# Routing of batch 0 beside the fourth to sixth attention group, and its scatters between GpSimd's masks

## The chip, the core and the metric

The kernel runs on one core of a Trainium2 chip. The core has TensorE (PE; PEld is its weight load), VectorE (DVE), ScalarE (ACT), GpSimd (POOL) and SyncE (SP), each with a queue of its own that it works through in order; they wait for each other by semaphores, and 16 DMA engines move data. The metric is the device time of one execution in microseconds.

## The reference

Two transformer blocks on x of 2 x 1024 tokens by 128 channels, all in float32. The change touches the first block alone:

```python
h = _layernorm(x, axis=-1) * (1 + ca) + sa
x = x + ga * _L0_attn_ref(h, ...)      # causal attention, 16 heads of 8
h = _layernorm(x, axis=-1) * (1 + cb) + sb
x = x + gb * _L0_ffn_ref(h, ...)       # mixture of experts
# in _L0_ffn_ref, T = 2048 tokens, E = 64 experts of 128 -> 64 -> 128:
scores = jax.nn.sigmoid(x @ gate_w.T) + gate_bias
group_scores = scores.reshape(T, 8, 8).max(axis=-1)
_, sel_groups = lax.top_k(group_scores, 4)
topk_w, topk_i = lax.top_k(scores * mask, 6)
topk_w = topk_w / (topk_w.sum(axis=-1, keepdims=True) + 1e-08)
# out = shared expert + sum over the 6 experts of topk_w * down(silu(gate) * up)
```

The second block is four RWKV layers and a small mixture of experts, and is the same in both kernels.

## The kernel before

**Attention.** Batch and heads are cut into NG = 8 groups of 4 heads: groups 0 to 3 are batch 0, 4 to 7 are batch 1. A group is NU = 24 units. A unit takes one block of 128 keys, two heads and one half (c = 0 or 1) of the queries: TensorE forms scores (L808), ScalarE exp into pt, a ring of four (L1066), GpSimd masks the diagonal block where there is one (`mask`, L725: units 0 to 7 and 16 to 23 of a group), and after each second unit TensorE multiplies with V (`outputs`, L824) for the pair of units before. Beside the units of one group run the row maxima of the next: 38 pieces ("fills") of TensorE (L786, L790), each reduced by VectorE (L1218). Pieces take turns in three PSUM banks (4, 5, 7): `ITEMS` lists all users of these banks in order, the place modulo 3 gives the bank, and `await_bank` makes TensorE wait until the item three places before has been read. The last maxima are those of group 7, and end at unit 163 (unit 24g + u counts through, 0 to 191).

**Routing.** Tokens are handled in chunks of 512: chunks 0, 1 are batch 0, chunks 2, 3 batch 1. For a chunk: `inverse` (ScalarE, 1/den by Ln and Exp), `normalise` (VectorE), `project` with WO (TensorE), `add_attention`, `centre`, `square`, `variances`, `rstds`, `modulated`, `logits`, `exponentials`, then on VectorE `route_scores`, `route_groups`, `route_mask`, `route_top`, `route_comb`, whose operations each wait for the one before (`link`); `turn_h` and `keep_h` transpose h to tokens. Per batch follow `positions` (on TensorE counts of tokens per expert and ranks; on VectorE each token's six slot rows), `experts_of_tiles`, and the scatter: 8 blocks x 6 indirect DMAs of 64 KB on GpSimd (L735) that write h rows to their slots in memory.

In the kernel before all of this for chunks 0 and 1 is written beside the units of group 7 (`beside`, `last_group`), `positions(0)` after attention, and the scatters of both batches behind the last mask in GpSimd's queue.

**After attention** come the rest of routing, the shared expert (L894 to L903, L1415, L1419), 16 `slot_weights` of three operations (L1386 to L1389) on VectorE, and the experts: 28 quads of 4 x 128 slots per batch. A quad passes through `turn_rows` (L910), `gates` (L924), silu, moe_hid (L1426), `turn_hidden` (L933) and `downs` (L941) in four successive steps. The loads of a batch's quads wait for all its 48 scatters. Then outputs are gathered (L746) and combined.

## Time and profile before

| | us |
|---|---|
| median of 3 runs (lowest, highest) | 1055.51 (1054.58, 1059.43) |
| profiled execution, its own time | 1065.52 |
| span of its trace | 1063.8 |
| TensorE busy (share) | 879.5 (83%) |
| VectorE | 726.7 (68%) |
| ScalarE | 565.1 (53%) |
| GpSimd | 252.4 (24%) |
| first exponential of group 7, last product of attention | 287.1, 324.4 |
| scatters, first and last start | 331.7, 455.0 |
| gathers, first and last start | 498.5, 648.1 |

How to read the rows below. A row of a window gives from:to, its length, the busy time of each engine it names with the number of instructions (x), then the granted TensorE clock as a share of 2.4 GHz, the share of the DMA engines and GB/s. A row of the timeline gives start, duration, engine, line, operation, output<-input with shapes and how many were merged (x), and in brackets how long the engine had been idle before it and what ended that; "issue" is a gap for which the profile shows no wait. A row by source line has the shortest, middle and longest duration in ns. Durations of matmuls overlap their successors.

### The profile page before, as it was taken

Reading aid. Unit: us, or ns where it says so; the run is one execution under the profiler, and the core shown is the slowest. Engines: PE = TensorE matmul, PEld = TensorE weight load, DVE = VectorE, ACT = ScalarE, POOL = GpSimd, SP = SyncE. Lnnn points to the kernel's source line nnn. Section 1 sums busy time; section 2 is a strip of 40 time slices with the busy share of each in tenths; the row PEclk is TensorE's granted clock in tenths of the full one; section 3 lists DMA queues with packets and bytes.
Section 4 is the critical chain, followed back from the end, with each engine's and each line's share of the span. In section 5 each row is a group of like instructions: output and inputs, shape, how many; then the busy total and the mean of one; then the engine's idle time right before and its main releaser. Section 6 shows DMA issues by size and latency. Waiting matters only on the chain. (4 is left out here: it accounts for less than half of the span.)

```text
span 1063.8 us, 13432 instructions
## 1 busy us (share of the span) xinstructions
PE 879.5 (83%) x4333; PEld 453.7 (43%) x4333; DVE 726.7 (68%) x1323; ACT 565.1 (53%) x888; POOL 252.4 (24%) x348
## 2 busy tenths in 40 slices
PE   6899999999885527998999003869999999998998
PEld 3453344444222216887888001324433433343433
DVE  4879788888476576332655133679889888996675
ACT  3325666666762103553554001668769868875743
POOL 1011122222114777711770674000000000000000
PEclk9889899999986577998999555989999999998999
DMA  2732655642022124654774211100000020000001
GB/s 86 225 69 52 185 161 168 194 145 69 12 65 89 49 72 158 228 182 153 216 227 138 64 52 57 33 0 1 10 23 10 1 52 1 0 1 0 1 0 40
DMA packets 51054, 87.48 MB, mean 82 GB/s; under 512 B 11202, under 2 KB 22832, under 8 KB 49200
## 3 DMA queue, kind: packets, MB, share of 16 engines
q1 hardware_dynamic: 36716, 58.56, 18.6%
q10 hardware_dynamic: 8128, 15.47, 4.0%
q0 software_dynamic: 6144, 12.60, 3.7%
q8 instruction: 38, 0.62, 0.2%
q14 instruction: 28, 0.23, 0.1%
HBM read 43.28 MB, written 40.89 MB: 79 GB/s over the span
## 5 line engine op out<-in xcount | busy, mean ns | idle before, releaser
L1066 ACT ACTIVATE pt<-psum 128x1024 f32<-128x1024 f32 (+1 forms) x192 | 149.9, 814 | 115.6 <-PE psum L808 115.2
L1218 DVE TENSOR_REDUCE part_max<-psum 128x1 f32<-128x512 f32 (+3 forms) x304 | 184.5, 657 | 35.7 <-PE psum L790 19.9
L786 PE MATMUL psum<-ka,qa 72*128 72x512 bf16 (+3 forms) x384 | 115.1, 341 | 5.3 <-DVE part_max L1218 1.8
L746 POOL DMA_INDIRECT part<-slot_y,slot_row x96 | 92.9, 968 | 100.1 <-DMA slot_y<-pt 71.5
L735 POOL DMA_INDIRECT slot_x<-va,slot_row x96 | 95.4, 994 | 37.5 <-issue 29.0
L725 POOL TENSOR_SCALAR_AFFINE_SELECT pt<-pt 128x256 f32<-128x256 f32 x128 | 51.9, 407 | 220.0 <-ACT pt L1066 219.3
L808 PE MATMUL psum<-qa,ka 75*128 75x512 bf16 (+3 forms) x384 | 96.3, 334 | 3.1 <-DMA qa<-neg_t 1.5
L1426 DVE TENSOR_TENSOR moe_hid<-moe_silu,psum 128x256 f32<-128x256 f32 x56 | 23.3, 418 | 95.8 <-ACT moe_silu L1186 91.4
L824 PE MATMUL psum<-pt,va_g 128*32 128x512 f32 (+3 forms) x768 | 84.1, 511 | 0.4 <-POOL pt L725 0.3
L110 ACT ACTIVATE ln_sq<-psum 128x512 f32<-128x512 f32 x44 | 26.1, 594 | 100.4 <-PE psum L93 100.3
L786 PEld LDWEIGHTS psum<-ka,qa 72*128 72x128 bf16 x384 | 37.4, 98 | 81.1 <-DVE part_max L1218 59.6
L1193 ACT COPY pt<-psum 128x512 f32<-128x512 f32 x56 | 32.8, 585 | 62.4 <-PE psum L941 62.4
L941 PE MATMUL psum<-ka,moe_hid_t 64*128 x448 | 64.2, 284 | 0.0
L924 PE MATMUL psum<-qa,xs_t 128*128 x448 | 63.0, 286 | 0.0
L1763 PE MATMUL psum<-mix_c,wt_c 128*128 128x512 f32 x128 | 61.1, 600 | 0.0
L941 PEld LDWEIGHTS psum<-ka,moe_hid_t 64*128 64x128 f32 x448 | 53.9, 187 | 10.9 <-issue 10.9
L101 PE MATMUL psum<-ln_sq,mean 128*128 128x512 f32 x88 | 49.1, 653 | 11.4 <-ACT ln_sq L110 11.4
L924 PEld LDWEIGHTS psum<-qa,xs_t 128*128 128x128 f32 x448 | 57.7, 202 | 0.6 <-issue 0.3
L1773 PE MATMUL psum<-kf,wt_c 128*128 128x512 f32 x128 | 57.9, 594 | 0.0
L948 PE MATMUL psum<-ident,va 128*128 128x128 f32 x16 | 3.3, 357 | 65.4 <-DVE va L1443 65.4
L910 PE MATMUL psum<-ident,pt 128*128 128x128 f32 x224 | 39.3, 303 | 20.8 <-DMA pt<-slot_x 20.8
L1720 PE MATMUL psum<-hp,wt_a 128*128 128x512 f32 x96 | 50.0, 602 | 2.7 <-issue 2.7
(316 smaller groups left out, 1658.2 us busy)
## 6 DMA issues: line engine op xcount, KB each, us to landing
slot_x<-zero ACTq DMA_DIRECT2D x8, 1792.0 KB, 6.7
pt<-slot_x SPq DMA_DIRECT2D x56, 256.0 KB
slot_y<-pt SPq DMA_DIRECT2D x56, 256.0 KB, 2.1
qa<-in_moe_gu SPq DMA_DIRECT2D x4, 1024.0 KB, 5.8
qa<-rows_q SPq DMA_DIRECT2D x21, 192.0 KB
ka<-rows_k SPq DMA_DIRECT2D x21, 192.0 KB
wt_c<-in_channel_w SPq DMA_DIRECT2D x4, 576.0 KB, 4.0
o_den<-acc SPq DMA_DIRECT2D x32, 64.0 KB, 2.3
```

Of the source, the lines that this page charges most:

```text
L725: pool.affine_select(out=pt[:, u % 4, :, 0:P], in_=pt[:, u % 4, :, 0:P], compare_op=ALU.is_ge, fill=0.0, base=0, pattern=[[0, 2], [1, P]], ...
L735: pool.indirect_dma_start(out=xs_d[b], out_offset=bass.IndirectOffsetOnAxis(ap=row[:, n, j:j + 1], axis=0), in_=h_tok[:, n, :], in_offset= ...
L746: pool.indirect_dma_start(out=yg[:, n % 4, j, :], out_offset=None, in_=ys_d[b], in_offset=bass.IndirectOffsetOnAxis(ap=row[:, n, j:j + 1], ...
L786: mm = pe.matmul(bank[:, nk * h:nk * (h + 1)], qa[0:ROWS, g % RING, h0 + h, chunk(i, P)], ka[0:ROWS, g % RING, h0 + h, k0:k0 + nk], start= ...
L808: mm = pe.matmul(out[:, 0:n], ka[0:ROWS + 3, g % RING, 2 * p + k, chunk(j, P)], qa[0:ROWS + 3, g % RING, 2 * p + k, q0:q0 + n], start=True ...
L824: mm = pe.matmul(acc_bank[32 * h:32 * h + 32, q0 - CH * c:CH], va_g[k][:, j, h, :], pt[:, 2 * (q % 2) + h // 2, h % 2, 0:n], start=(j == 0 ...
L924: mm = pe.matmul(gu_bank[n % 2][:, chunk(k, P)], xs_t[:, n % 2, chunk(k, P)], gu_w[:, bass.ds(held[n][k], P)], start=True, stop=True)
L941: mm = pe.matmul(y_bank[n % 2][:, chunk(k, P)], hid_t[:, n % 2, chunk(k, P)], down_w[:, bass.ds(held[n][k], P)], start=True, stop=True)
L1066: act.activation(pt[:, u % 4, :, 0:n], score_bank[u % 2][:, :, 0:n], ACT.Exp, scale=SCALE)\
L1218: dve.tensor_reduce(part_max[:, h0:h0 + heads, slot], bank_of("fill", f)[:, 0:heads * nk].rearrange("p (h n) -> p h n", h=heads), AX_X, AL ...
L1763: pe.matmul(G.bank[6 + j % 2][:, :], wt_c[u // 2 % 2][:, WCK + j, :], mix_c[:, 0, q, :], start=True, stop=True)\
L1773: mm = pe.matmul(G.bank[4 + q][:, :], wt_c[u // 2 % 2][:, WCV + j, :], kf[:, j, q, :], start=(j == 0), stop=(j == 3), skip_group_check=True)
```

## The change

Batch 0 is routed beside groups 3 to 5. A table STEP_AT gives each of its 13 TensorE steps a unit (90 to 136), and the steps are entered in ITEMS, so that they take their turns in the banks of the row maxima; `await_bank` learns what frees each. VectorE and ScalarE have a `first_batch(unit)` with their parts of each step. ScalarE copies the centred chunk out of its bank first (one copy of 128x512 more for chunks 0 and 1). `positions` is split into `tile_ends`, `slot_keys` and `slot_rows`. GpSimd issues one scatter of batch 0 in each of the units 134 to 181, behind that unit's mask if there is one. `slot_weights` moves into the experts of batch 0, one in each second step.

```diff
+    EARLY = NU * 3
+    STEP_AT = {("project", 0): EARLY + 18, ("centre", 0): EARLY + 20, ("variance", 0): EARLY + 22, ("logits", 0): EARLY + 25,
...
+    SCATTER_AT = EARLY + 62
...
-        ITEMS += [("fill", f) for f in BACK[unit]]
+        ITEMS += [("fill", f) for f in BACK[unit]] + [item for item, at in STEP_AT.items() if at == unit]
...
+            if was == "project":
+                pe.wait_ge(x_new, k + 1)
+            if was == "centre":
+                pe.wait_ge(ln.squared, n0 + k + 1)
+                pe.wait_ge(centre_kept, k + 1)
+            if was == "variance":
+                pe.wait_ge(ln.logged, n0 + k + 1)
...
@@ GpSimd
+                        if 0 <= NU * g + u - SCATTER_AT < INDEXED:
+                            scatter(0, NU * g + u - SCATTER_AT)
-                for b in range(B):
-                    scatter(b)
+                for k in range(NU * NG - SCATTER_AT, INDEXED):
+                    scatter(0, k)
+                for k in range(INDEXED):
+                    scatter(1, k)
...
@@ TensorE, group(g)
+                        first_batch(unit)
                         beside(unit - NU * LAST)
...
                 def after_attention():
 
-                    positions(0)
+                    pe.wait_ge(v_in, NG)
                     turn_h(2)
-                    turn_experts(0)
                     project(3)
...
@@ ScalarE
+                    if c < 2:
+                        act.copy(G.h[:, chunk(c)], centre_bank[c][:, :]).then_inc(centre_kept, 1)
...
@@ VectorE
+                def first_batch(unit):
+
+                    for c in range(2):
+                        if unit == STEP_AT["project", c] - 1:
+                            normalise(c)
+                        if unit == STEP_AT["project", c]:
+                            add_attention(c)
+                        if unit == STEP_AT["variance", c] + 1:
+                            modulated(c)
+                        if unit == STEP_AT["logits", c] + 1:
+                            route_scores(c)
+                        if unit == STEP_AT["logits", c] + 4:
+                            route_groups(c)
+                        if unit == STEP_AT["logits", c] + 6:
+                            route_mask(c)
+                        if unit == STEP_AT["logits", c] + 8:
+                            route_top(c)
+                        if unit == STEP_AT["logits", c] + 10:
+                            route_comb(c)
+                    if unit == STEP_AT["count", 0]:
+                        tile_ends(0)
+                    if unit == STEP_AT["rank", 0]:
+                        slot_keys(0)
+                    if unit == SCATTER_AT - 2:
+                        slot_rows(0)
...
                 def after_attention():
 
-                    positions(0)
-                    experts_of_tiles(0)
                     route_scores(2)
...
-                    for n in range(NT):
-                        slot_weights(n)
...
                                 keep_hidden(n - 2)
+                            if not b and step % 2:
+                                slot_weights(step // 2)
```

GpSimd's queue in the kernel before, from the masks of group 6 on (affine_select is the mask, DMA the scatter or gather):

```order
L725 AFFINE_SELECT pt<-pt 128x2x128 x16
L718 COPY va_g<-va 128x256
L725 AFFINE_SELECT pt<-pt 128x2x128 x24
L735 DMA slot_x<-va,slot_row 14336x128 x96
L746 DMA part<-slot_y,slot_row 128x128 x96
```

The same queue in the changed kernel, from the copy of V in group 5 on:

```order
L746 COPY va_g<-va 128x256
L763 DMA slot_x<-va,slot_row 14336x128 x2
L753 AFFINE_SELECT pt<-pt 128x2x128
L763 DMA slot_x<-va,slot_row 14336x128
L753 AFFINE_SELECT pt<-pt 128x2x128
L763 DMA slot_x<-va,slot_row 14336x128
L753 AFFINE_SELECT pt<-pt 128x2x128
```

A scatter stands behind each mask; 16 such pairs, then nine scatters in a row, 16 pairs, and the last scatters follow.

VectorE's queue in the kernel before in group 4, where the row maxima (L1218) of the next group follow each other:

```order
L1248 COPY neg_t<-psum 96x128
L1218 TENSOR_REDUCE part_max<-psum 128x1 x12
L1218 TENSOR_REDUCE part_max<-psum 128x4
L1218 TENSOR_REDUCE part_max<-psum 128x1 x4
L1218 TENSOR_REDUCE part_max<-psum 128x2 x2
L1218 TENSOR_REDUCE part_max<-psum 128x1 x16
```

The same place in the changed kernel (row maxima are L1254), units 95 to 101:

```order
L1284 COPY neg_t<-psum 96x128
L1254 TENSOR_REDUCE part_max<-psum 128x1 x7
L1321 SCALAR_TENSOR_TENSOR h<-h,mod,ln_rs 128x512
L1324 TENSOR_SCALAR h<-h,mod 128x512
L1254 TENSOR_REDUCE part_max<-psum 128x1 x4
L1339 TENSOR_SCALAR score<-score 128x256
L1340 RECIPROCAL score<-score 128x256
L1341 TENSOR_TENSOR score<-score,gate_bias 128x256
L1254 TENSOR_REDUCE part_max<-psum 128x1
L1254 TENSOR_REDUCE part_max<-psum 128x4
L1254 TENSOR_REDUCE part_max<-psum 128x1 x3
L1346 TENSOR_REDUCE gmax<-score 128x4x8
```

Two to three operations of the routing now stand between every few maxima.

## Rows read from the trace of the kernel before

**Rows 1.** windows, all engines: a steady group, the stretches of routing, group 7, experts

```profile
170.50:199.20 28.70, 28.67 (x233) 11.80 (x225) 24.43 (x45) 19.38 (x27) 7.07 (x17) 1.00 0.57 182
...
190.20:246.60 56.40, 56.34 (x446) 23.45 (x448) 47.94 (x87) 37.84 (x52) 13.74 (x33) 1.00 0.44 135
...
297.50:324.40 26.90, 22.69 (x133) 7.79 (x133) 18.64 (x83) 17.18 (x25) 3.20 (x8) 0.86 0.02 7
...
416.00:494.00 78.00, 78.00 (x624) 69.71 (x623) 26.75 (x53) 39.32 (x76) 30.56 (x32) 1.00 0.55 184
```

**Rows 2.** timeline, between attention's end and the experts' first steps

```profile
328.84 0.63 ACT L1082 ACTIVATE rden<-rden 128x512 f32<-128x512 f32 x1
...
333.85 0.69 DVE L1252 TENSOR_TENSOR o_den<-o_den,rden 128x512 f32<-128x512 f32 x1
...
381.81 0.75 DVE L1419 SCALAR_TENSOR_TENSOR x<-psum,mod,x 128x512 f32<-128x512 f32 x1 [1.22 <-PE psum L903]
...
411.56 1.06 PE L933 MATMUL psum<-ident,moe_hid 128*64 128x128 f32 x4 [7.89 <-DVE moe_hid L1426]
...
415.97 1.21 PE L941 MATMUL psum<-ka,moe_hid_t 64*128 x8
...
419.03 1.16 PE L941 MATMUL psum<-ka,moe_hid_t 64*128 x8
```

**Rows 3.** timeline of GpSimd, and its scatters by source line

```profile
190.21 0.41 POOL L725 TENSOR_SCALAR_AFFINE_SELECT pt<-pt 128x256 f32<-128x256 f32 x1 [0.51 <-ACT pt L1066]
...
246.60 0.41 POOL L725 TENSOR_SCALAR_AFFINE_SELECT pt<-pt 128x256 f32<-128x256 f32 x1 [11.16 <-ACT pt L1066]
...
263.45 0.64 POOL L718 COPY va_g<-va 128x256 f32<-128x256 f32 x1
...
296.86 0.47 POOL L725 TENSOR_SCALAR_AFFINE_SELECT pt<-pt 128x256 f32<-128x256 f32 x1 [0.35 <-ACT pt L1066]
...
333.13 0.97 POOL L735 DMA_INDIRECT slot_x<-va,slot_row  x1 [0.30 <-issue]
...
L735 POOL DMA_INDIRECT slot_x<-va,slot_row x96: 963/967/1457, 331.7 to 455.0; - x96
```

**Rows 4.** windows and timeline of VectorE: routing, row maxima, steps of a chunk

```profile
297.08:305.67 8.59, 8.05 (x40) 1.00 0.12 32
...
325.00:331.36 6.36, 5.20 (x25) 0.77 0.66 231
...
261.74 5.92 DVE L1218 TENSOR_REDUCE part_max<-psum 128x1 f32<-128x512 f32 x10
...
275.52 0.69 DVE L1218 TENSOR_REDUCE part_max<-psum 128x1 f32<-128x512 f32 x1 [0.38 <-PE psum L790]
...
278.10 0.68 DVE L1252 TENSOR_TENSOR o_den<-o_den,rden 128x512 f32<-128x512 f32 x1
...
282.20 0.75 DVE L1274 SCALAR_TENSOR_TENSOR x<-psum,mod,x 128x512 f32<-128x512 f32 x1 [3.42 <-PE psum L840]
...
293.18 0.75 DVE L1281 SCALAR_TENSOR_TENSOR h<-psum,mod,ln_rs 128x512 f32<-128x512 f32 x1 [7.50 <-ACT ln_rs L1096]
...
293.97 0.49 DVE L1284 TENSOR_SCALAR h<-h,mod 128x512 f32<-128x512 f32 x1
```

**Rows 5.** timeline of TensorE in group 7

```profile
309.11 1.10 PE L840 MATMUL psum<-o_den,wo_t 128*128 128x512 f32 x2 [2.64 <-DVE o_den L1252]
```

**Rows 6.** timeline of VectorE: slot weights, and its idle time in the experts

```profile
382.47 0.55 DVE L1386 TENSOR_TENSOR same_key<-slot_key,top_key 128x384 f32<-128x384 f32 x1
...
384.24 0.56 DVE L1386 TENSOR_TENSOR same_key<-slot_key,top_key 128x384 f32<-128x384 f32 x1
...
425.12 0.42 DVE L1426 TENSOR_TENSOR moe_hid<-moe_silu,psum 128x256 f32<-128x256 f32 x1 [1.99 <-ACT moe_silu L1186]
```

**Rows 7.** windows of TensorE alone, in groups 0 and 1

```profile
76.00:79.00 3.00, 2.33 (x22) 1.00 0.03 6
...
106.00:109.00 3.00, 1.76 (x11) 0.99 0.53 136
```

More of the change, by code:

```diff
@@ L493, in stage_core @@
     FRONT[8], BACK[8] = beside_unit[8], []
+    EARLY = NU * 3
+    STEP_AT = {("project", 0): EARLY + 18, ("centre", 0): EARLY + 20, ("variance", 0): EARLY + 22, ("logits", 0): EARLY + 25,
+               ("turn_h", 0): EARLY + 27, ("project", 1): EARLY + 36, ("centre", 1): EARLY + 38, ("variance", 1): EARLY + 40,
+               ("logits", 1): EARLY + 44, ("turn_h", 1): EARLY + 46, ("count", 0): EARLY + 56, ("rank", 0): EARLY + 57,
+               ("experts", 0): EARLY + 64}
+    SCATTER_AT = EARLY + 62
     ITEMS = [("fill", f) for f in range(HEAD - 3)] + [("turn", 0)] + [("fill", f) for f in range(HEAD - 3, HEAD)]
@@ L862, in turn_h, with counts @@
                     mm.then_inc(turned, 1)
-                def positions(b):
+                def counts(b):
                     pe.wait_ge(picked_done, 2 * b + 2)
                     pe.wait_ge(const_done, 4)
-                    pe.wait_ge(prob_done, NU * NG)
                     tiles = range(BLOCKS * b, BLOCKS * (b + 1))
@@ L873, in positions, with ranks @@
                     mm.then_inc(count_psum, 1)
+                def ranks(b):
+                    tiles = range(BLOCKS * b, BLOCKS * (b + 1))
                     pe.matmul(rank_bank[b][:, :], earlier[:, :], picked[:, tiles[0]:tiles[-1] + 1, :].rearrange("p n e -> p (n e)"),
@@ L983, in beside @@
                     if w == 19:
-                        pe.wait_ge(exp_done, 2)
                         variances(2)
-                    if w == 21:
-                        pe.wait_ge(h_kept, 1)
-                        turn_h(1)
                     if w == 23:
                         logits(2)
+                def first_batch(unit):
+                    for c in range(2):
+                        if unit == STEP_AT["project", c]:
+                            await_bank(pe, "project", c)
+                            project(c)
+                        if unit == STEP_AT["centre", c]:
+                            await_bank(pe, "centre", c)
+                            centre(c)
+                        if unit == STEP_AT["variance", c]:
+                            await_bank(pe, "variance", c)
+                            variances(c)
+                        if unit == STEP_AT["logits", c]:
+                            await_bank(pe, "logits", c)
+                            logits(c)
+                        if unit == STEP_AT["turn_h", c]:
+                            await_bank(pe, "turn_h", c)
+                            pe.wait_ge(v_in, NG // 2)
+                            turn_h(c)
+                    if unit == STEP_AT["count", 0]:
+                        await_bank(pe, "count", 0)
+                        counts(0)
+                    if unit == STEP_AT["rank", 0]:
+                        await_bank(pe, "rank", 0)
+                        ranks(0)
+                    if unit == STEP_AT["experts", 0]:
+                        await_bank(pe, "experts", 0)
+                        turn_experts(0)
                 def group(g):
@@ L1020, in after_attention @@
                     turn_h(3)
-                    positions(1)
+                    pe.wait_ge(prob_done, NU * NG)
+                    counts(1)
+                    ranks(1)
                     turn_experts(1)
@@ L1145, in beside, with first_batch @@
                         rstds(2)
-                    if w == 22:
-                        keep_h(1)
+                def first_batch(unit):
+                    for c in range(2):
+                        if unit == STEP_AT["project", c] - 2 - 2 * c:
+                            inverse(c)
+                        if unit == STEP_AT["centre", c]:
+                            square(c)
+                        if unit == STEP_AT["variance", c]:
+                            rstds(c)
+                        if unit == STEP_AT["logits", c]:
+                            exponentials(c)
+                        if unit == STEP_AT["turn_h", c]:
+                            keep_h(c)
                 def group(g):
@@ L1269, in group @@
                         fills(BACK[unit])
+                        first_batch(unit)
                 def add_attention(c):
@@ L1467, in after_attention @@
                     route_comb(3)
-                    positions(1)
+                    tile_ends(1)
+                    slot_keys(1)
+                    slot_rows(1)
                     experts_of_tiles(1)
```

132 lines of the change are left out of this document (53 added, 79 removed).

## The prediction

> **What bounds the kernel now.** I read the engines' busy time by stage first, then the timeline around the joints of the stages, then one line at a time. A group of attention takes 28.7 us in its steady part, and TensorE is busy for 28.67 of it, at the full clock of 2.4 GHz (granted 1.00); VectorE is busy 24.43 and GpSimd 7.07 [rows 1]. So TensorE bounds groups 2 to 6, but VectorE has only 4.3 us of air in each. Group 7 has no row maxima left, and its last 16 units (297.5 to 324.4) are slower than TensorE's work asks: 22.69 busy of 26.90 [rows 1]. After attention comes the stretch in which nothing is near full: 324.4 to 416, where TensorE waits for the routing of chunk 3, then for the scatters of batch 0 (48 on GpSimd, then 48 of batch 1), and at last 7.89 us for moe_hid, because VectorE is still at the 16 slot weights [rows 2]. The first down projection starts at 415.97, and from there the experts run at 3.0 us a quad with TensorE 78.00 of 78.00 busy [rows 1, 2]. All that follows (batch 1, its gathers, the RWKV layers) hangs on that start. The question is thus: what does the change do to the end of attention, and to the distance from there to the first down projection.
>
> I count units through: unit 24g + u. A unit with a mask shows its time by GpSimd's mask: unit 89 at 190.21, unit 136 at 246.60, unit 175 at 296.86 [rows 3].
>
> **Part A, units 89 to 136: batch 0's routing beside the row maxima.** This window is 56.4 us now, TensorE 56.34 busy, VectorE 47.94 [rows 1]. What VectorE gets on top, for each of two chunks: the multiplication by 1/den 0.68, add_attention 0.75, modulated 0.75 + 0.49 and the small gaps, together 2.7; the routing chain 8.59 (it has links: each piece waits for the one before) [rows 4]. That is 5.4 + 17.2. Then counts, keys, rows and experts_of_tiles: 6.36 with a wait of 0.7 in it, so 5.6, and 0.3 to keep the expert numbers. Sum 28.5. With 47.9 this is 76.4 us of VectorE in a window of 56.4. Against it stand two things: maxima that now stand alone with 0.69 run at 0.592 when they queue (5.92 for ten) [rows 4], which I put at 2 us in the window; and VectorE's waits for the steps it shares with the others (13 banks of the ring of three go to steps, each held until ScalarE or VectorE has read it, and add_attention, modulated, the counts and the ranks are waited for in order), some 0.3 us each, 4 us. The ring lets TensorE be only three banks, about 1.8 us, ahead of VectorE, so a chain of 2.6 us that stands in one unit can't be hidden and must be paid out of the 4.3 us a group. Result 76.4 - 2 + 4 = 78.4, that is +22. TensorE's own new work here is six products of 128x512 at 1.10 [rows 5], and for transposes, logits, counts and ranks (an estimate from the same row by their columns) some 3 us, less what overlaps: about 9.2 us, and it lies under VectorE's. ScalarE, with 19.38 busy of 28.70 in a group [rows 1], has room for its eight operations of about 0.6 a chunk. Ends: if packing gave 4 us and no step waited, +16; if TensorE's 9.2 stood in series with VectorE's 76.4, +29. I take +22, by the busy row.
>
> **Part B, units 136 to 175: GpSimd.** Now 50.3 us from mask to mask (296.86 - 246.60). GpSimd then has, between these two starts, 39 scatters, 31 masks and one copy of V. A scatter is 0.967 and starts 0.30 after the one before, 1.27 in all; a mask is 0.41, the copy 0.64 [rows 3]. 39 x 1.27 + 31 x 0.41 + 0.64 = 62.9, +12.6. GpSimd becomes the bound here: masks are waited for by the output products, the pt ring holds four units, and TensorE and ScalarE can't run past it; in the eight units without a mask GpSimd still needs 10.2 for eight scatters and starts them late, so it gets no rest there. No row shows a mask next to a scatter. From below: the 0.30 vanishes when something else is in between, 39 x 0.97 + 13.3 = 51.1, +0.9. From above: mask and copy also get 0.30 behind them, 32 x 0.30 = 9.6 more, +22. I take 1.27 and 0.41, as both stand in rows.
>
> The Trainium skill (GPSIMD Engine Reference, section 2.1 Instruction dispatch) says that a Pool core starts its share of the next instruction as soon as it has done its own of the one before; by that rule alone the lower end, +0.9, would be the sum. It is a rival below, priced by rows.
>
> **Part C, units 176 to the end of group 7.** Routing of chunks 0 and 1 is gone from here. TensorE idles 4.2 us in 26.9 [rows 1]; 2.64 of it is the wait for the product with 1/den of chunk 2, which VectorE reached late because of chunk 1's chain [rows 5]; the transposes of chunks 0 and 1 go too. The clock falls to 1.2 GHz in this group now, behind that stall (0.86 granted in the window [rows 1]), and I expect one fall with the change too, behind the slow first half of the group. -4.5; ends 0 and -7.
>
> **Part D, end of attention to first down projection.** VectorE no longer starts with positions and experts of batch 0. The next thing in the way is 1/den of chunk 3: ScalarE ends it at 328.84 + 0.63 = 329.5, and it hangs on a DMA of the last accumulator, so it doesn't move; VectorE used it at 333.85 [rows 2]. So the chain of chunk 3 (project, centre, variance, logits, routing, rows, shared expert) moves by 4.35, not by the 6.4 removed. The shared expert's last addition, 381.81 + 0.75 = 382.6, comes at 378.2. Then TensorE can start on the experts at once: scatters of batch 0 are out before attention ends, the quads are loaded, and the slot weights have moved into the loop. Three steps to the first down projection: at most 3 x 3.06 (415.97 to 419.03 [rows 2]), less since the first steps are short; I take 8. 386.2 against 415.97: -29.8. Ends -27 (steps at 1.2 GHz) and -32. What covers the slot weights: three operations in 1.77 us (382.47 to 384.24) every second step, in VectorE's idle of 1.99 before moe_hid [rows 6]; if this cover failed by 0.5 us a time it would cost 7. Batch 1's scatters start with its rows, 4.35 earlier, last 61, and are done at half of batch 0's experts (28 x 3.0 = 84), so no new wait follows; the 39 us that they ran beside the experts until now (416 to 455 [rows 3]) left the steps at 3.0. Everything behind keeps its length.
>
> **Sum.** +22.0 + 12.6 - 4.5 - 29.8 = +0.3 us. The profiled execution took 1065.52 (span 1063.8); with the change 1065.8. The runs' median is 1055.51, 10 lower; moved by the same, 1055.8, say 1056. About 0.5% (5.3 us) is what a measurement of this kernel can tell from no change.
>
> **The rivals.**
> 1. Forecast: the two new bounds (VectorE to unit 136, GpSimd after it) eat what the earlier start gives. 1050 to 1063 by the ends of A alone. 0.40.
> 2. Mask and scatter overlap: 0.97 + 0.41 a pair. B is +0.9 instead of +12.6, 1056 - 11.7 = 1044. For it: a gap that is issue may lie under a mask that runs. Against it: each scatter behind another has its 0.30, as issue time and not as a wait [rows 3]. 0.22. The rule of the Trainium skill above would give this one.
> 3. Row maxima and routing share VectorE better than I think, and only TensorE's 9.2 us count in A: 1056 - 12.8 = 1043. Against it stand 76.4 us of work in 56.4. 0.10.
> 4. Slower: every GpSimd instruction carries the 0.30, a pair costs 1.98 us in units 136 to 175, which is 9.6 more: 1066. It decides from a mean of some 1.85 us a pair. 0.20.
> 5. Slower by the clock: in Part B TensorE is busy about 0.7 of the time in group 6. Rows show it staying at 1.00 with 2.33 of 3.00 busy, and falling after a stretch with 1.76 of 3.00 [rows 7]. At 1.2 GHz a unit with maxima costs 2 x 28.67 / 24 = 2.4 us, above GpSimd's 1.68; two such episodes of 6 us cost 6: 1062. 0.08.
>
> The chances: faster by over 0.5%: 2 and 3 nearly whole (0.29) and a little of 1 (0.03), 0.32. Slower: 4 and 5 (0.25) and 0.04 of 1, 0.29. Within: 0.39. The range, 1042 to 1068, reaches to the rivals on both sides; the likeliest case has 1050 to 1063 for itself.
>
> **What would show it.** A: mask of unit 136 (the first mask behind two scatters) near 269 instead of 246.6, VectorE over 90% busy before it and maxima without waits. B: 63 us from there to the last mask of group 7's first half, GpSimd above 90% busy, start of scatter to start of the next in masked units 1.68; 1.4 or 2.0 speaks for 2 or 4. A granted clock of 0.5 in group 6 speaks for 5. C and D: last output product near 354, first down projection near 416, and no wait for moe_hid at it. I am wrong if the first down projection moves by more than 5 us in either direction, or if steps of the experts with slot weights take over 3.1 us.

## The result and the profile after

The changed kernel takes 1068.46 us (median; 1064.76 the lowest) against 1055.05 for the kernel before on the same chip: ratio 1.0101, 95% interval [1.0057, 1.0146]. Medians here and below are of all executions, while ratios leave out those in a second, slower state (here one of the changed kernel, 1082.46 us), so a ratio isn't the quotient of the two medians. The changed kernel is slower by about 1%, which is 10.7 us; on the 1055.51 of the prediction that makes 1066, inside the range and near its upper end of 1068. The sum had said no change.

The profiled execution of the changed kernel took 1066.5 us (span 1064.8), 1.0 more than that of before (1065.52). The traces differ by less than the times because the profiled execution of before was a long one (1065.52 against a median of 1055). A second profile of the kernel before (run e0 below) took 1062.0. Both have stretches that the other lacks, and I give both. The places are those of the prediction, read from the timeline of GpSimd (masks) and of TensorE (products):

| stretch, us | before | e0 | after | forecast against before | measured against before, e0 |
|---|---|---|---|---|---|
| A, mask of unit 89 to that of 136 | 56.4 | 56.4 | 87.7 | +22 | +31.3, +31.3 |
| B, unit 136 to 175 | 50.3 | 50.2 | 60.0 | +12.6 | +9.8, +9.8 |
| C, unit 175 to the last output product | 27.0 | 24.0 | 23.0 | -4.5 | -4.0, -1.0 |
| D, from there to the first down projection | 92.1 | 89.0 | 59.7 | -29.8 | -32.4, -29.3 |
| from there to the end | 647.8 | 645.0 | 647.0 | 0 | -0.8, +2.0 |
| start to unit 89 | 190.2 | 195.7 | 187.3 | 0 | -2.9, -8.3 |
| from unit 89 to the end | 873.6 | 864.6 | 877.5 | +0.3 | +3.9, +12.9 |

The row "start to unit 89" is not the change's: both programs do the same up to there. The windows from mask 16 to mask 32 (group 1) show it, of before, of e0 and of after (columns as in [rows 1]):

```profile
109.00:141.90 32.90, 32.74 (x237) 12.83 (x235) 26.30 (x48) 19.87 (x27) 7.07 (x17) 0.90 0.51 158
```

```profile
106.40:147.40 41.00, 40.60 (x239) 14.91 (x238) 27.09 (x49) 20.40 (x27) 7.10 (x18) 0.72 0.42 128
```

```profile
107.80:137.90 30.10, 29.67 (x238) 12.09 (x237) 26.00 (x48) 19.53 (x27) 7.09 (x18) 1.00 0.56 174
```

The same 16 masks and the same work take 30 to 41 us, by how long the granted clock stays at 0.50 after the opening of group 1: not at all in after, from about 109 to 116 in before, from 106 to 128 in e0. In the profiles below the stretch goes up to 44.1 us. This alone can move the time of one execution by some 14 us, so a single profile's total says little here. I compare stretches from unit 89 on, and times by their medians.

Windows of after, all engines: A, B, C (to 358.5), D, and the experts.

```profile
187.33:275.02 87.69, 77.15 (x479) 30.49 (x480) 72.89 (x198) 46.36 (x65) 16.67 (x35) 0.86 0.27 85
275.02:335.06 60.04, 47.77 (x326) 16.88 (x323) 27.70 (x52) 30.36 (x43) 51.67 (x72) 0.83 0.31 102
335.06:358.50 23.44, 21.62 (x116) 6.22 (x116) 2.68 (x4) 15.73 (x22) 10.61 (x16) 0.78 0.08 29
358.50:417.78 59.28, 33.24 (x113) 16.40 (x112) 32.84 (x124) 12.56 (x22) 19.73 (x20) 0.68 0.26 83
...
417.80:495.80 78.00, 78.00 (x623) 69.72 (x624) 48.26 (x94) 39.47 (x76) 28.64 (x28) 1.00 0.55 183
```

The first answers to 190.20:246.60 of [rows 1]. TensorE was busy 56.34 of 56.40 there; now it isn't full (77.15 of 87.69), VectorE isn't either (72.89 of 87.69), and the clock is down to 0.86. In the second GpSimd is the fullest, 51.67 of 60.04. The last is as before, steps of 3.0 us with the slot weights in them. What the engines waited for in A, first TensorE, then VectorE (line waited at, releaser, us in all, times, longest):

```profile
PE psum L818 <- DVE part_max L1254: 7.4, 11, 2.1
PE psum L867 <- DVE part_max L1254: 1.3, 1, 1.3
PE psum L902 <- DVE part_max L1254: 1.1, 1, 1.1
...
DVE part_max L1254 <- PE psum L822: 7.5, 11, 1.8
DVE part_max L1254 <- PE psum L818: 3.0, 4, 1.7
DVE slot_key L1403 <- PE psum L912: 1.4, 1, 1.4
DVE x L1311 <- PE psum L872: 1.0, 1, 1.0
```

In turns each of the two waits for the other: TensorE for a bank of the ring to be read, VectorE for one to be filled. Before, TensorE had no such wait in A, and VectorE 7.6 us of them, all for maxima. Of VectorE's 12.9 us of waits now, 10.5 are for maxima (part_max) and 2.4 for the moved steps (slot_key, x).

GpSimd's timeline at the start of B, which answers to [rows 3]:

```profile
271.22 1.17 POOL L763 DMA_INDIRECT slot_x<-va,slot_row  x1 [12.96 <-DVE slot_row L1420]
272.70 0.97 POOL L763 DMA_INDIRECT slot_x<-va,slot_row  x1 [0.30 <-issue]
275.02 0.40 POOL L753 TENSOR_SCALAR_AFFINE_SELECT pt<-pt 128x256 f32<-128x256 f32 x1 [1.35 <-ACT pt L1105]
275.59 0.98 POOL L763 DMA_INDIRECT slot_x<-va,slot_row  x1 [0.16 <-issue]
276.59 0.42 POOL L753 TENSOR_SCALAR_AFFINE_SELECT pt<-pt 128x256 f32<-128x256 f32 x1
277.18 0.98 POOL L763 DMA_INDIRECT slot_x<-va,slot_row  x1 [0.17 <-issue]
...
328.71 0.41 POOL L753 TENSOR_SCALAR_AFFINE_SELECT pt<-pt 128x256 f32<-128x256 f32 x1
329.29 0.98 POOL L763 DMA_INDIRECT slot_x<-va,slot_row  x1 [0.17 <-issue]
330.30 0.41 POOL L753 TENSOR_SCALAR_AFFINE_SELECT pt<-pt 128x256 f32<-128x256 f32 x1
330.88 0.98 POOL L763 DMA_INDIRECT slot_x<-va,slot_row  x1 [0.17 <-issue]
```

Scatter behind scatter starts after its 0.30 as before; from scatter to scatter with a mask between is 1.59 (275.59 to 277.18): the mask starts without a gap behind the scatter, and 0.16 to 0.17 stands between mask and scatter. In all of B, behind its first mask, GpSimd waits for another engine once, for 0.17 us.

TensorE's granted clock falls in B too, and stays at 0.50 from about 315, in group 6, to about 345. One window of it:

```profile
316.00:343.00 27.00, 22.23 (x104) 5.28 (x104) 0.00 (x0) 12.72 (x19) 23.00 (x31) 0.50 0.34 113
```

The pairs keep to 1.59 us ahead of this fall and inside it (329.29 to 330.88), so up to unit 175 it added no time to what GpSimd's queue took.

And the joints of C and D, of ScalarE, VectorE, TensorE and GpSimd, which answer to [rows 2, 5, 6]:

```profile
362.45 0.63 ACT L1121 ACTIVATE rden<-rden 128x512 f32<-128x512 f32 x1
...
363.19 0.69 DVE L1288 TENSOR_TENSOR o_den<-o_den,rden 128x512 f32<-128x512 f32 x1 [1.17 <-ACT rden L1121]
...
392.00 0.98 POOL L763 DMA_INDIRECT slot_x<-va,slot_row  x1 [34.70 <-DVE slot_row L1420]
...
410.56 0.75 DVE L1481 SCALAR_TENSOR_TENSOR x<-psum,mod,x 128x512 f32<-128x512 f32 x1 [1.22 <-PE psum L938]
...
417.78 1.13 PE L976 MATMUL psum<-ka,moe_hid_t 64*128 x8
420.75 1.16 PE L976 MATMUL psum<-ka,moe_hid_t 64*128 x8
423.75 1.16 PE L976 MATMUL psum<-ka,moe_hid_t 64*128 x8
```

VectorE now takes up 1/den of chunk 3 at 363.19, 0.1 us after ScalarE has it (363.08); before it came 4.35 later. From the last addition of the shared expert (410.56 + 0.75) to the first down projection are 6.5 us, before 33.4 (382.56 to 415.97).

### The profile page after: what moved, and what is told of

It reads as the page before. It is cut to its first block and busy times, and to the rows that moved or that the text cites. A ratio compares the mean times of both kernels' runs of the same rounds, so it can differ in the third digit from the quotient of the medians.

```text
span 1064.8 us, 13451 instructions
## 1 busy us (share of the span) xinstructions
PE 889.5 (84%) x4333; PEld 451.7 (42%) x4333; DVE 724.8 (68%) x1323; ACT 568.8 (53%) x890; POOL 253.8 (24%) x348
## 5 line engine op out<-in xcount | busy, mean ns | idle before, releaser
L1254 DVE TENSOR_REDUCE part_max<-psum 128x1 f32<-128x512 f32 (+3 forms) x304 | 184.9, 658 | 39.1 <-PE psum L822 21.0
L818 PE MATMUL psum<-ka,qa 72*128 72x512 bf16 (+3 forms) x384 | 118.0, 346 | 12.8 <-DVE part_max L1254 9.4
L840 PE MATMUL psum<-qa,ka 75*128 75x512 bf16 (+3 forms) x384 | 101.8, 356 | 2.7 <-DMA qa<-neg_t 1.5
L856 PE MATMUL psum<-pt,va_g 128*32 128x512 f32 (+3 forms) x768 | 90.2, 544 | 11.6 <-POOL pt L753 8.6
L840 PEld LDWEIGHTS psum<-qa,ka 75*128 75x128 bf16 x384 | 35.2, 104 | 41.8 <-issue 16.1
```

The lines of the kernel that those rows point to most:

```text
L818: mm = pe.matmul(bank[:, nk * h:nk * (h + 1)], qa[0:ROWS, g % RING, h0 + h, chunk(i, P)], ka[0:ROWS, g % RING, h0 + h, k0:k0 + nk], start= ...
L840: mm = pe.matmul(out[:, 0:n], ka[0:ROWS + 3, g % RING, 2 * p + k, chunk(j, P)], qa[0:ROWS + 3, g % RING, 2 * p + k, q0:q0 + n], start=True ...
L856: mm = pe.matmul(acc_bank[32 * h:32 * h + 32, q0 - CH * c:CH], va_g[k][:, j, h, :], pt[:, 2 * (q % 2) + h // 2, h % 2, 0:n], start=(j == 0 ...
L1254: dve.tensor_reduce(part_max[:, h0:h0 + heads, slot], bank_of("fill", f)[:, 0:heads * nk].rearrange("p (h n) -> p h n", h=heads), AX_X, AL ...
```

## The experiments

The theory after this reading of the trace: A costs 31 because VectorE's added work can't fill VectorE's idle time, and B is GpSimd's. Rivals for A: bursts longer than the ring of three, the fallen clock, the handovers of the moved steps. All runs are timed against the kernel before on the same chip.

**e0, the kernel before again.**

> The kernel before, unchanged, for a second profiled execution and for the ratio of a kernel to itself. The profiled execution of before lay 10.0 us over the median of its timed runs (1065.52 against 1055.51), that of the changed kernel at its median (1066.5), so the two traces alone differ by 1.0 us where the times differ by 13. Theory 1: those 10 us are one place or a few in that execution (a stretch at a lower granted clock or a late transfer) and a new profile near 1055 lacks them: unit 89's mask to unit 136's then is below 56.4 us, or the head's first 190.2 us shorter. Theory 2: a profiled execution is always some 10 us longer than a timed one: the new profile is at 1065 again with all stretches as before. Ratio of times 1.000 within 0.005 by both.

Ratio 1.0 [0.9979, 1.0021]; median 1059.36, profiled 1062.01. The ratio came as expected, and neither theory holds whole. The long stretches aren't one place: group 1 is another 8.1 us longer than in the first profile, C and D 3 us shorter each.

**e2, no scatter beside a mask.** GpSimd's loop alone:

```diff
+                free_units = [n for n in range(SCATTER_AT, NU * NG) if 8 <= n % NU < 16]
-                        if 0 <= NU * g + u - SCATTER_AT < INDEXED:
-                            scatter(0, NU * g + u - SCATTER_AT)
-                for k in range(NU * NG - SCATTER_AT, INDEXED):
+                        if NU * g + u in free_units:
+                            scatter(0, free_units.index(NU * g + u))
+                for k in range(len(free_units), INDEXED):
```

> The changed kernel with batch 0's scatters only in units that have no mask (8 to 15 of a group, from unit 134 on: 18 of them), the other 30 behind the last mask, in the 34.7 us in which GpSimd is idle there (357.3 to 392.0). Theory 1 (pair): a mask and a scatter one behind the other take 1.585 us and set the pace of the masked units, so this gives back the 9.8 us that units 136 to 175 grew by (60.0 to about 50 us): about 1057 to 1059, ratio to the kernel before 1.001. Theory 2 (clock): those units are slow because TensorE's granted clock was 0.83 there and 0.50 in group 7, whatever GpSimd does: the stretch stays at 57 us or more, the total within 3 us of 1068. By both the first down projection moves by less than 3 us on account of the scatters themselves, since 30 x 1.27 = 38 us fit nearly into the idle 34.7.

Median 1047.91, ratio 0.9885 [0.9844, 0.9927]: faster than both kernels, and twice what was expected. A and B of its profile:

```profile
188.12:278.02 89.90, 80.07 (x479) 31.30 (x480) 72.96 (x198) 46.39 (x65) 16.63 (x36) 0.83 0.27 82
278.02:320.50 42.48, 40.45 (x322) 15.22 (x321) 26.87 (x52) 29.31 (x42) 20.85 (x41) 1.00 0.22 70
```

B falls from 60.0 to 42.5, below the 50.3 of before, and the clock in it is 1.00 in place of 0.83. So the pairs cost 17.5 us in B, and 2.0 more in C (21.0). The difference to before, 7.8, is what batch 0's routing had cost there and the change had taken away; behind the pairs it couldn't be seen. Theory 2 falls for B: with the pairs gone the clock doesn't fall, so its fall there was a consequence of them. D is 59.5: the 30 late scatters hold nothing up.

**e1, all scatters behind the last mask.** 

```diff
-                        if 0 <= NU * g + u - SCATTER_AT < INDEXED:
-                            scatter(0, NU * g + u - SCATTER_AT)
-                for k in range(NU * NG - SCATTER_AT, INDEXED):
+                for k in range(INDEXED):
```

> The changed kernel with all 48 scatters of batch 0 behind the last mask, none beside the masks, so that GpSimd in units 134 to 191 has what it had before the change. By the run e2, the pairs of mask and scatter cost 17.5 us in units 136 to 175: without any scatter there the stretch is at 42 to 43 us, as in e2, and the next one at 21. Then the scatters of batch 0 take 48 x 1.27 = 61 us from about 340 on, to 401, past the 392 at which GpSimd began with batch 1 in the changed kernel, and batch 0's first expert steps start when the last has landed: first down projection at 401 + 8 to 12 = 409 to 413, against 401.00 in e2. Total 1056 to 1060, ratio 1.000. Rival: the experts' start isn't held by the scatters but by VectorE's chain for batch 1, and the first down projection stays at 401 to 403, total 1048, ratio 0.990.

Median 1061.63, ratio 1.005 [1.002, 1.0079]. B is 42.3, C 20.3, the first down projection 408.68, D 72.8 (59.5 in e2). TensorE's timeline ahead of it:

```profile
401.06 1.94 PE L943 MATMUL psum<-ident,pt 128*128 128x128 f32 x8 [14.21 <-DMA pt<-slot_x]
...
408.68 1.13 PE L974 MATMUL psum<-ka,moe_hid_t 64*128 x8
```

As the first expectation has it, and not its rival: B and C are those of e2, and GpSimd's queue costs 14.2 us of waiting at the other end. D is worth its whole only while batch 0's scatters are out early enough; 18 of 48 in free units are enough (e2), and so are 10 (e8 below, where the last 38 follow the masks).

**e3, the kernel before with the slot weights moved, and nothing else.**

```diff
-                    for n in range(NT):
-                        slot_weights(n)
+                            if not b and step % 2:
+                                slot_weights(step // 2)
+                        if not b:
+                            slot_weights(NT - 1)
```

> The kernel before with one thing of the change alone: the 16 slot weights of VectorE are computed one by one inside batch 0's 32 expert steps, not before them. Theory 1: they stand on the path to the first step (the chain of TensorE's turns of rows, the copies of VectorE behind the weights), some 8.5 us of them: the first down projection comes at about 407.5 in place of 415.97 and the whole is 8 us shorter, ratio 0.992, about 1047. Theory 2: VectorE's own slack in a step is too small, the 16 steps that hold a slot weight grow by its 0.5 us each, and what is saved ahead is given back: ratio 1.000 within 0.003.

Median 1046.88, ratio 0.9882 [0.986, 0.9904]. D is 80.3 against 92.1 and 89.0. Its down projections:

```profile
403.68 1.13 PE L941 MATMUL psum<-ka,moe_hid_t 64*128 x8
406.65 1.16 PE L941 MATMUL psum<-ka,moe_hid_t 64*128 x8
409.65 1.16 PE L941 MATMUL psum<-ka,moe_hid_t 64*128 x8
```

The steps stay at 3.0. Some 9 to 12 us of D's 29 to 32 need no early routing at all, and this smallest part of the change is by itself as good, within the intervals, as the best of all runs here.

**e4, VectorE's chain in pieces.** Same work, one piece of about 1 us a unit:

```diff
-                        if unit == STEP_AT["logits", c] + 1:
-                            route_scores(c)
-                        if unit == STEP_AT["logits", c] + 4:
-                            route_groups(c)
...
+                        pieces = [scores_1, lambda c: scores_2(c, 0), lambda c: scores_2(c, 1), scores_3, groups_1, groups_2,
+                                  mask_1, mask_2, top_1, top_2, comb_1, comb_2]
+                        if 0 <= unit - STEP_AT["logits", c] - 1 < len(pieces):
+                            pieces[unit - STEP_AT["logits", c] - 1](c)
```

> The changed kernel with the same instructions of VectorE, but the routing chain of batch 0 cut into pieces of at most about 1 us, one piece a unit (the score block's reciprocal of 1.4 us in two halves, groups, mask, top, combination, keys and rows in two parts each). Theory 1 (bursts): the rotating banks hold three fills, a burst of 2 to 3 us of VectorE outlasts them, TensorE stops up to 2.2 us and its granted clock falls to 0.5 to 0.66 in places, after which VectorE waits for TensorE (14.8 us idle against the 4 forecast); spread out, the waits go, the clock in units 89 to 136 is at 0.95 or more, and the stretch falls from 87.7 to about 77 us: total about 1058, ratio 1.002. Theory 2 (total work): VectorE's added 24 us set the stretch and the idle time is due to the order of the fills: the stretch stays at 85 to 88 us and the ratio at 1.010.

Median 1071.09, ratio 1.0125 [1.0085, 1.0165]; A is 87.2 (87.7), TensorE's longest wait there 1.3 in place of 2.1 us, and the clock as low as in the changed kernel, 0.86. The burst theory falls: the longest wait is shorter, but TensorE's waits for VectorE are 10.1 us in all where they were 10.4.

**e7, VectorE's work alone.** The kernel before, its routing where it was, and stand-ins for the moved instructions of VectorE in units 89 to 136:

```diff
+                def stand_in(unit):
...
+                        if at == logits + 1:
+                            link(dve.tensor_scalar(sc, sc, 1.0, None, ALU.add))
+                            link(dve.reciprocal(sc, sc))
+                            link(dve.tensor_tensor(sc, sc, G.gate_bias[:, :].unsqueeze(1).to_broadcast([P, 4, E]), ALU.add))
+                        if at == logits + 4:
+                            route_groups(c)
...
                         fills(BACK[unit])
+                        stand_in(unit)
```

> The kernel before, with its own routing where it was, and besides in units 89 to 136 instructions of VectorE that stand in for the moved ones: same kinds, sizes and units (about 24 us), on tiles that are written again later, without any wait for TensorE, ScalarE or GpSimd. Theory 1 (VectorE's total work, with what TensorE's clock makes of it): the stretch from unit 89's mask to unit 136's grows from 56.4 to 85 us or more as in the changed kernel (87.7); total 1087 or more, ratio 1.028. Theory 2 (the chain of handovers): it is the waits of the moved steps for one another across TensorE, ScalarE and VectorE that cost the 15 us beyond VectorE's own work; without them the stretch is at 70 to 76 us, total 1073 to 1078, ratio 1.017.

Median 1091.69, ratio 1.033 [1.0285, 1.0375]. A:

```profile
194.91:278.73 83.82, 76.31 (x446) 27.36 (x448) 72.50 (x192) 39.31 (x52) 14.64 (x33) 0.76 0.30 91
```

The same 446 products of TensorE as in [rows 1] and none of the moved ones, and still +27.4 of the +31.3. By this comparison TensorE's own new work and the handovers of the steps together are worth 3.9. B, C and D are 50.2, 25.6 and 88.9, untouched. TensorE's clock fell to 0.76 here with nothing added but VectorE's load, and it takes part in the 27.4, as two windows of 16 us in this A show:

```profile
194.91:210.91 16.00, 13.19 (x112) 5.72 (x110) 15.30 (x30) 8.10 (x13) 5.21 (x12) 1.00 0.47 108
260.91:276.91 16.00, 15.75 (x53) 3.92 (x52) 10.62 (x25) 6.84 (x8) 0.00 (x0) 0.50 0.02 8
```

At a granted 1.00 VectorE is nearly full, 15.30 of 16.00. At 0.50 TensorE is, 15.75 of 16.00, with less than half as many products, and VectorE is idle for 5.4 us. e7 at a held clock was not run.

**e6 and e9, the clock held up.** e2 with two (e6) or one (e9) unread products of 128 columns ahead of the scores of units 89 to 135:

```diff
+                    if 89 <= NU * g + u < 136:
+                        keep_busy(pe, G, score_bank[u % 2][:, 0, :], 2)
```

> The kernel of the run e2 (batch 0's scatters in the units without a mask) with two more multiplications of TensorE (128 columns, 0.33 us each in the kernel before, whose results nobody reads) ahead of the scores of each of the units 89 to 135. Theory 1 (clock): the stretch from unit 89's mask to unit 136's is 89.9 us there, though VectorE has only 73 us of work in it, because TensorE stands for moments and its granted clock then is 0.50 to 0.80 for 5 to 15 us at a time; with the gaps partly filled the clock is at 0.95 or more and the stretch falls to 78 to 82 us, 1038 to 1042 in all, ratio 0.980. Theory 2 (TensorE's time counts as well): 94 multiplications add 20 to 30 us of TensorE's time to a stretch in which it is busy 88% of the time; the clock is higher and the stretch is no shorter, or longer (90 to 100 us), ratio 0.990 to 1.000.

> The kernel of the run e2 with one multiplication (128 columns, result unread) ahead of the scores of each of the units 89 to 135, where the run e6 had two. In e6 the granted clock was 1.00 throughout and the stretch still 91.0 us, with TensorE busy 87.7 of it: 94 such multiplications took the place of the slow clock. With 47 of them TensorE's work at full clock is 56.3 + some 3 for the added steps + 47 x 0.31 = 74 us. Theory 1 (the fallen clock costs 8 to 12 us of the 31): the stretch from unit 89's mask to unit 136's falls from 89.9 to 78 to 82 us at a clock of 0.95 or more, total about 1038 to 1041. Theory 2 (the clock follows VectorE's load and costs little by itself; the idle time of VectorE is the handover of each fill, about 10 us in any case): the stretch stays at 86 to 90 us, total 1045 to 1049.

Medians 1048.64 and 1042.33, ratios 0.9928 [0.9901, 0.9954] and 0.9861 [0.9822, 0.9899]. A of e6, then of e9:

```profile
185.80:276.82 91.02, 87.71 (x674) 51.86 (x677) 73.51 (x199) 46.87 (x66) 16.50 (x36) 1.00 0.26 82
```

```profile
200.14:285.92 85.78, 78.35 (x577) 40.90 (x574) 72.67 (x198) 46.19 (x66) 16.80 (x35) 1.00 0.28 86
```

Both hold the granted clock at 1.00 for all of A. In e6 the products take all that the clock gives: TensorE is busy 87.71 of 91.02. In e9 A is 4.1 shorter than in e2 (89.9), not the 8 to 12 that theory 1 expected, and VectorE is still idle for 13.1 us. At 1.00 throughout, +29.4 are left of the 31. But the 4.1 is net of what the 47 products themselves take from TensorE, which no run shows apart, so it isn't the clock's whole price. The cleaner evidence that most of the 31 isn't the clock comes from e8 and e11 below, whose clock in A stays near 1.00 without such products.

**e8 and e10, chunk 1 later.** e2 with the steps of chunk 1, counts, ranks and experts 24 units later; e10 also has one unread product a unit in units 96 to 111 and 136 to 155.

```diff
-               ("turn_h", 0): EARLY + 27, ("project", 1): EARLY + 36, ("centre", 1): EARLY + 38, ("variance", 1): EARLY + 40,
-               ("logits", 1): EARLY + 44, ("turn_h", 1): EARLY + 46, ("count", 0): EARLY + 56, ("rank", 0): EARLY + 57,
+               ("turn_h", 0): EARLY + 27, ("project", 1): EARLY + 60, ("centre", 1): EARLY + 62, ("variance", 1): EARLY + 64,
+               ("logits", 1): EARLY + 68, ("turn_h", 1): EARLY + 70, ("count", 0): EARLY + 80, ("rank", 0): EARLY + 81,
...
-    SCATTER_AT = EARLY + 62
+    SCATTER_AT = EARLY + 86
```

> The kernel of the run e2 with the routing of batch 0's second chunk, the ranks and the experts of tiles 24 units later (from unit 132 on, first scatter from unit 158; 10 scatters in units without a mask, 38 behind the last mask). Theory 1 (the rate of VectorE's work decides): before, VectorE is busy 85% in these units, so 24 us more in 47 units overfill it, but 12 in each half fit better and the last third meets group 7, where no row maxima are left: the stretch to unit 136 is 70 to 75 us in place of 89.9, that from 136 to 175 grows from 42.5 to 50 to 55, and the sum of both falls by 5 to 10 us; 38 scatters end by about 390, and the first down projection isn't held up by them. Total 1038 to 1043, ratio 0.983. Theory 2 (what is moved costs the same wherever it is put beside row maxima): the sum of the two stretches stays at 130 to 134 us, and the total at 1048 or, with the scatters late, above it.

> The kernel of the run e8 (second chunk's routing 24 units later) with one such multiplication ahead of the scores of the units 96 to 111 and 136 to 155, where its clock fell to 0.50 for some 10 us each time (213 to 218 us and 272 to 282 us). Theory 1 (the fallen clock costs time): the two stretches, 69.9 and 58.8 us there, fall together by 5 to 8 us, total about 1039 to 1041. Theory 2: what the 36 multiplications take (some 11 us of TensorE) is what the clock gives back; sum of both stretches within 2 us of 128.7, total 1045 to 1048.

e8: median 1046.46, ratio 0.9905 [0.9872, 0.9938], A 69.9 and B 58.8, sum 128.7 against 132.4 in e2. e10: median 1051.19, ratio 0.9926 [0.9891, 0.9961], sum 129.7. A with half of the work is +13.5 over before, for 9.9 us more of VectorE's time, at a granted 0.95:

```profile
187.71:257.64 69.93, 65.15 (x450) 26.04 (x450) 57.84 (x130) 43.55 (x62) 14.20 (x34) 0.95 0.34 104
```

The rest turned up in B. The sum fell by 3.7 where 5 to 10 were expected, and the time is that of e2 within the intervals. 38 scatters behind the masks held nothing up (D 60.1), as expected. For e10 theory 2 holds in the sum (within 2 us of 128.7); its median lies 3 us above the 1045 to 1048 expected.

**e11 and e12, other units for the chain.** e2 with logits at units 103 and 127 in place of 97 and 116, and what follows later as well; e12 with one unread product a unit besides.

```diff
-    STEP_AT = {("project", 0): EARLY + 18, ("centre", 0): EARLY + 20, ("variance", 0): EARLY + 22, ("logits", 0): EARLY + 25,
+    STEP_AT = {("project", 0): EARLY + 18, ("centre", 0): EARLY + 20, ("variance", 0): EARLY + 22, ("logits", 0): EARLY + 31,
...
-               ("logits", 1): EARLY + 44, ("turn_h", 1): EARLY + 46, ("count", 0): EARLY + 56, ("rank", 0): EARLY + 57,
+               ("logits", 1): EARLY + 55, ("turn_h", 1): EARLY + 57, ("count", 0): EARLY + 68, ("rank", 0): EARLY + 69,
```

> The kernel of the run e2 with the routing behind the logits at other units: chunk 0's from unit 104 on (before: 98), chunk 1's from 128 on (before: 117), so that each falls on units 8 to 15 of a group, where VectorE was idle for 2.2 of 11.8 us in the kernel before (206.4 to 218.2) against 0.9 of 7.2 in the first eight units; counts, ranks and experts 12 units later, first scatter at unit 152. Theory 1 (place): VectorE's idle time lies where TensorE sets the pace, and the steps of e2 stand where VectorE does; moved, they fill it, and the two stretches from unit 89 to unit 175, 132.4 us in e2, are at 124 to 128, total about 1042. Theory 2 (total): what the steps take is added wherever they stand among row maxima, at 1.1 to 1.4 us for each us of VectorE's work; the sum stays at 130 to 135, total 1046 to 1050.

> The same with one multiplication of 128 columns ahead of the scores of each of the units 89 to 135, as in the run e9. In e9 they held the granted clock at 1.00 and the stretch from unit 89 to 136 went from 89.9 to 85.8 us, the median from 1047.9 to 1042.3 us, by an interval that doesn't tell the two apart. Theory 1: the fallen clock costs 4 to 5 us, whatever the units of the steps: this run is 4 to 5 us below e11's. Theory 2: the multiplications give nothing, and it is within 2 us of e11's.

e11: median 1049.46, ratio 0.9881 [0.9847, 0.9914]; its profile has A + B at 125.9, as theory 1 said, but the ratio equals e2's 0.9885. e12: 1050.63, 0.9929 [0.9886, 0.9972], A + B 137.0 in a profile at much the same places. Two profiles 11 us apart and two ratios that overlap: this pair tells nothing on the place, and against e9 it leaves open whether the unread products gain anything. The A of each, e11 then e12:

```profile
201.75:274.29 72.54, 65.78 (x468) 27.27 (x472) 63.87 (x164) 45.24 (x66) 14.46 (x34) 0.98 0.32 100
```

```profile
183.95:269.85 85.90, 80.12 (x564) 42.37 (x565) 66.66 (x169) 45.86 (x66) 14.25 (x33) 0.94 0.27 85
```

e11's A grew by 16.1 over before, for 15.9 us more of VectorE's time, with the clock at 0.98: near the full clock too, none of the idle time took up work.

## Why the prediction was right or wrong

The sum said +0.3 and the kernel became 10.7 us slower. That the time still lay inside the range is the width of the range: its upper part was there for rivals 4 and 5, and what made the kernel slower was neither.

**Part A failed, in one term.** VectorE's work was priced well: forecast 74.4 (76.4 less 2), measured 72.89. What failed is "VectorE's waits for the steps it shares with the others, 4 us": that sum lets VectorE run full but for these 4, and so let 8.5 us of its idle time (56.4 - 47.9) swallow part of the new work. Measured idle: 14.8 us, more than before. The waits for the shared steps were even shorter than priced, 2.4 us; the waits for maxima, which the sum put at nothing (7.6 before), were 10.5. The runs bear out that the idle time isn't owed to the steps: e7 has 11.3 idle with no step at all, e9 13.1 at full clock, e8 12.1 with half the work. VectorE's busy share in A was 85.0% before, 83.1% after, and in the runs without unread products 81.2% (e2), 82.6% (e4), 86.5% (e7), 82.7% (e8) and 88.0% (e11); with unread products 80.8% (e6), 84.7% (e9), 79.3% (e10) and 77.6% (e12). Had I left the share where it was, 74.4 / 0.85 = 87.5 us would have stood there; the time was 87.7. Some luck is in so close a hit: with the measured 72.89 it gives 85.8, and the shares spread by several points. My upper end, +29, came from another mechanism (TensorE's 9.2 in series) and was too low too; e7 shows that without TensorE's new work +27.4 are reached.

Why the share stays near there is only argued: stretches in which TensorE sets the pace (217 to 227 us of after, TensorE 5.00 of 5.00 and VectorE 3.0 to 4.0 of 5.00) alternate with others in which VectorE does, and three banks don't carry the slack of one into the next. In part these are stretches of a low clock (the windows of e7 above; the granted clock is 0.79 in 217 to 222 and 1.00 in 222 to 227). Summed over windows of 1 us, 8.4 of VectorE's 14.8 idle us in A of after fall in the 59.7 us at a granted 1.00, and 6.5 in the other 28; in e7 3.2 in 40.8, and 8.2 in the other 43. e4 excludes that it is the length of single bursts; e11 was to show the alternation and didn't decide it.

**Part B was right for the time and silent on the worth.** 62.9 forecast, 60.0 measured, the pair at 1.59 in place of 1.68; 31 pairs at 0.09 less are the whole difference. The pair lies between the lower end of 1.38 and the forecast, and masked units in a row run at GpSimd's pace. Rival 2 (0.97 + 0.41 a pair, 1044) is wrong: of the 0.30 only 0.13 to 0.14 goes. The Trainium skill (GPSIMD Engine Reference, section 2.1 Instruction dispatch) lets a core go on at once with the next instruction; the trace agrees for a mask behind a scatter (276.59 starts with no gap) and disagrees for the scatter behind a mask, which starts 0.16 to 0.17 later. What I didn't see is that +12.6 was reckoned from a stretch which, with the routing gone, would have shrunk to 42.5. Against that the pairs cost 17.5 in B, not 9.8. The prediction gave the gain of the removed routing to C alone.

**Part C.** -4.5 forecast; -4.0 by the first profile, -1.0 by the second, because before's own C varies from 24.0 to 27.0. The one expected fall of the clock came, earlier and longer: 0.50 from about 315, in group 6, to about 345, in group 7.

**Part D was right**, -29.8 against -32.4 and -29.3, with its steps: some 4.3 on chunk 3's chain, slot weights covered in the steps (3.0 us each), no wait for moe_hid. e3 splits it: 9 to 12 for the weights, some 21 for the early routing (80.3 to 59.7), and e1 adds the condition that the scatters be early.

**Rivals 3, 4 and 5.** 3 is excluded by A. 4's pair of 1.98 wasn't there (1.59), although its total, 1066, is that of the result. 5's sign came, a granted clock of 0.50 in group 6, but not its price: GpSimd's pairs set the pace through it. The clock fell in A already, which 5 didn't name; held at 1.00 there, A was 4 us shorter (e9), with what the unread products took already in that.

**The whole.** Forecast +0.3; from unit 89 on +3.9 and +12.9 by the two profiles of before; +10.7 for the whole kernel by the ratio. A's 9.3 too few is the largest single error; B (2.8 too many) and D (2.6 too many by the first profile, 0.5 too few by the second) partly hid it. The prediction's own sign of being wrong, a first down projection moved by over 5 us, didn't show: 417.78 against 415.97. But it was counted from the start, where group 1 was 2.8 us shorter after than before; counted from unit 89 it is +4.7, and against e0 +10.9.

**The changed kernel can be mended**: e2 (0.9885) turns it from 1% slower to 1% faster by taking 32 scatters from beside the masks. It is no better than e3 (0.9882), which leaves batch 0's routing where it was: the early routing gives some 21 us in D (80.3 in e3, 59.5 in e2) and 11 to 14 in B and C, and takes 31 to 34 in A. The lowest median is e9's 1042.33; its interval (0.9861 [0.9822, 0.9899]) overlaps with both.

## What to carry to other kernels

When work is added to an engine that trades buffers with another through a short ring, take as a first estimate its new total divided by the busy share that it had (in this kernel the share stayed within 81 to 88% where nothing else was added); don't let its idle time absorb the work, unless a run has shown that it can. When a change both removes work from a stretch and adds some, price each against the stretch without the other: a new bound can hide a gain that a small move (here of the scatters) sets free. And try the smallest part of a change by itself: moving the slot weights alone (0.9882) was worth as much as the whole change after mending (0.9885).

## What the hardware showed that was not expected

- One event before the changed code moves the time of this kernel by up to some 14 us: in group 1 the granted clock is at 0.50 for anything from no time (after) to some 30 us (e9), and the same 16 masks span 29.9 (e2) to 44.1 us.

```profile
106.60:150.70 44.10, 43.83 (x240) 15.47 (x238) 27.29 (x49) 20.50 (x27) 7.11 (x18) 0.67 0.40 119
```

That is e9, whose profiled execution was 16 us over its median. Since this fall lasts differently in executions of one program (before and e0), totals of single profiles weren't used.

- TensorE's clock can be brought down by another engine's load alone: in e7 it had the same 446 products in A as before and was granted 0.76, against 1.00. TensorE waited there for banks that VectorE hadn't read yet, 7.4 us in all and 1.8 at the longest, where it hadn't waited before.
- An indirect DMA on GpSimd has 0.30 us behind it when another follows, none when a mask follows (276.59 in the changed kernel), and 0.16 to 0.17 ahead of it when a mask stands there.
